# Graph attention and feed-forward, second aggregation: one fp32 product or three products of high and low parts

## The reference

```python
def gat_layer(x, W, att_src, att_dst, bias, src, dst, heads, out_ch, concat):
    h = (x @ W.T).reshape(n, heads, out_ch)
    e = leaky_relu(a_src[src] + a_dst[dst], 0.2)
    ex = jnp.exp(e - segment_max(e, dst)[dst])
    alpha = ex / (segment_sum(ex, dst)[dst] + 1e-16)
    out = segment_sum(alpha[:, :, None] * h[src], dst)
    return out + bias
x = x + gnn(layernorm(x))     # gat 1 (8 x 128), relu, gat 2 (1 x 768)
x = x + ffn(layernorm(x))     # gelu(x @ fc1.T + b) @ fc2.T + b; rows 0 to 5: gated atoms
```

## Time and profile before

| | us |
|---|---|
| median of 3 runs | 778.19 (777.96 to 779.61) |
| profiled execution | 781.36 |
| its span | 779.3 |
| PE busy | 743.4 (95%) |
| DVE busy | 525.1 (67%) |
| ACT busy | 365.4 (47%) |
| POOL busy | 79.1 (10%) |
| granted TensorE clock, mean share of full | 0.989 |

### The profile page before, as it was taken

How to read it: one execution, slowest core, us unless ns; L and a number is a source line. 1 busy time by engine, 2 the same in 40 slices (tenths; PEclk the granted TensorE clock), 3 DMA queues, 4 the chain that set the end, 5 groups by cost and what they waited for, 6 DMA issues and landing times.

```text
span 779.3 us, 12480 instructions
## 1 busy us (share of the span) xinstructions
PE 743.4 (95%) x4367; PEld 629.5 (81%) x4367; DVE 525.1 (67%) x944; ACT 365.4 (47%) x688; POOL 79.1 (10%) x94
## 2 busy tenths in 40 slices
PE   2889999969999999999999899999999999999998
PEld 1769999859899999999999799998567675666755
DVE  6999889498999999999999422253573505813141
ACT  4332434257788888888888811113122222221101
POOL 2011211000000000000000100000322502313010
PEclk9999999998999999999999999999999999999999
DMA  8335656659031112312410130005904038114001
GB/s 295 122 105 150 181 153 196 167 151 339 2 99 34 67 34 66 99 32 67 136 59 0 32 75 1 0 1 165 324 28 142 21 114 281 35 39 163 0 21 60
DMA packets 39770, 78.94 MB, mean 101 GB/s; under 512 B 4057, under 2 KB 25500, under 8 KB 38829
## 3 DMA queue, kind: packets, MB, share of 16 engines
q1 hardware_dynamic: 34057, 60.60, 25.6%
q10 hardware_dynamic: 4484, 13.82, 5.3%
q0 software_dynamic: 1184, 3.92, 2.0%
HBM read 63.04 MB, written 15.29 MB: 101 GB/s over the span
## 4 chain that ended last, share of the span: by engine, by line
PE 92%; DVE 4%; issue 2%; ACT 1%; DVEq 1%; DMA 0%; SPq 0%; ACTq 0%; POOL 0%; POOLq 0%
PE bank L1079 22%; PE bank L1219 17%; PE bank L1060 11%; PE bank L1148 11%; PE bank L992 11%; PE bank L1264 5%; PE bank L1284 4%; PE bank L918 2%; PE bank L1201 1%; PE bank L1095 1%; PE bank L1236 1%; PE bank L1252 1%; PE bank L1299 1%; PE bank L933 1%; PE bank L920 1%
## 5 line engine op out<-in xcount | busy, mean ns | idle before, releaser
L1079 PE MATMUL bank<-PT,h1s 125*128 125x250 f32 x800 | 176.0, 375 | 0.0
L1079 PEld LDWEIGHTS bank<-PT,h1s 125*128 125x128 f32 x800 | 149.0, 190 | 15.6
L1219 PE MATMUL bank<-h,PT 125*125 125x384 f32 x400 | 132.0, 487 | 0.0
L1604 DVE SCALAR_TENSOR_TENSOR L<-asb,nadh 125x1250 f32<-125x1250 f32 x80 | 118.0, 1517 | 7.1 <-PE bank L1060 5.3
L728 ACT COPY PT<-bank 125x500 f32<-125x500 f32 x200 | 100.1, 596 | 40.5 <-PE bank L1060 40.5
L1219 PEld LDWEIGHTS bank<-h,PT 125*125 125x125 f32 x400 | 74.2, 188 | 50.7 <-issue 0.7
L1612 DVE CUSTOM_DVE_ANT_0 L<-L,LC 125x1250 f32<-125x1250 f32 x80 | 113.4, 1456 | 0.0
L715 ACT ACTIVATE L<-L,nm 125x1250 f32<-125x1250 f32 x80 | 107.7, 1370 | 2.1 <-DVE nm L1616 2.1
L1060 PEld LDWEIGHTS bank<-ident,L 125*125 125x125 f32 x800 | 95.4, 192 | 7.5 <-ACT L L715 4.8
L1060 PE MATMUL bank<-ident,L 125*125 125x125 f32 x800 | 96.6, 277 | 4.9 <-ACT L L715 4.6
L1449 DVE TENSOR_TENSOR hotr<-iota,r 125x1500 f16<-125x1500 f16 x50 | 46.7, 935 | 3.1 <-issue 3.1
(11 more groups left out here) (222 smaller groups left out, 1048.1 us busy)
## 6 DMA issues: line engine op xcount, KB each, us to landing
asb<-src_logit_rows SPq DMA_DIRECT2D x7, 1250.0 KB, 6.0
atom_w<-in_atom_inT SPq DMA_DIRECT2D x5, 1152.0 KB, 14.0
atom_w<-in_atom_outT SPq DMA_DIRECT2D x5, 1152.0 KB, 7.5
log_count_scratch<-LCw SPq DMA_DIRECT2D x10, 546.9 KB
LC<-log_count_scratch SPq DMA_DIRECT2D x10, 546.9 KB
LCt<-log_count_scratch SPq DMA_DIRECT2D x10, 546.9 KB
h_scratch<-h1st ACTq DMA_DIRECT2D x10, 448.0 KB
h1s<-h_scratch SPq DMA_DIRECT2D x7, 560.0 KB
```

Of the source, the lines that this page charges most:

```text
L1079: mm = pe.matmul(bank[2 + (k - lag) % 2][:, 0:GW], h1s[q][:, s, :], PT[(k - lag) % 2][:, s, :], start=(s == 0), stop=(s == NT - 1))
L1219: mm = pe.matmul(bank[2 + 2 * j + b][0:NP, 0:HALF], PT5[:, s, j * NP:(j + 1) * NP], h2[:, s, b * HALF:(b + 1) * HALF], start=(s == 0), sto ...
L1604: dve.scalar_tensor_tensor(L[r][:, :], asb[q][0:NP, 1, :], nadh[q][:, t:t + 1], asb[q][0:NP, 0, :], ALU.add, ALU.max).then_inc(stt_done, 1)
```

## The change

The second aggregation is split like the projection. `h2_out` writes `h2_hi` (fp32r, ScalarE, both halves) and `h2_lo` (VectorE, the difference, both halves); `evac_5` writes `PT5_hi`, and VectorE's new `lower_5` writes `PT5_lo` from the same bank. Each (i, j, b) is now ten products high by high, ten high by low, ten low by high (`add_5`, `half_5`); for j = b = 0 they are interleaved with the transposes (`first_half_5`), which use other banks (`T5BANK`). In exchange for the room the low parts take, there is one `LCt` and one `x5` in place of two each, the outputs are summed in place in `x2f` (no `ost`), `tok_y` is gone (gate_logits reads y5), and `gp`, `bo`, `cw` share one place, with pads and other tiles moved. Logits, exponentials, count loads and x5 loads go by tile instead of by group, and stores by tile. `bo` is loaded after five steps of the gate; its bias is added in `gate_weights`, no more in `add_route`. In the diff below, of rewritten functions the new lines stand; the old ones are in the code above.

```diff
-T5BANK = [2, 3, 0, 1, 3]
+T5BANK = [0, 1, 3, 0, 1]
...
-        h2 = sb("h2", [NP, NT, D], F32, two_ctx)
-        PT5 = sb("PT5", [NP, NT, GW], F32, two_ctx)
+        h2_hi = sb("h2_hi", [NP, NT, D], F32R, two_ctx)
+        x5 = sb("x5", [NP, D], F32, two_ctx)
...
-        scr = sb("scr", [NCLS, D], F32, two_ctx)
-        tok_y = sb("tok_y", [NCLS, D], F32, two_ctx)
+        atom_w.append(sb("atom_w2", [128, KD * FH], F32, two_ctx))
+        gT = sb("gT", [128, KF, GW], F32, two_ctx)
...
-        LCt = [sb(f"LCt{j}", [NP, N], F32, p4) for j in range(2)]
+        LCt = sb("LCt", [NP, N], F32, p4)
-        x5 = [sb(f"x5_{j}", [NP, D], F32, p4) for j in range(2)]
+        h2_lo = sb("h2_lo", [NP, NT, D], F32R, p4)
+        PT5_hi = sb("PT5_hi", [NP, NT, GW], F32R, p4)
+        PT5_lo = sb("PT5_lo", [NP, NT, GW], F32R, p4)
-        ost = [sb(f"ost{j}", [NP, D], F32, p4) for j in range(2)]
...
+            def lc_load(n):
+                if n > 0:
+                    sp.wait_ge(max5, n)
+                for a, b in ROWS:
+                    sp.dma_start(LCt[a:b, :], lc_d[n * NP + a:n * NP + b, :]).then_inc(lct_in, 16)
+            def out_store(i, j):
+                first = NCLS if i == j == 0 else 0
+                t = 2 * i + j
+                sp.wait_ge(out_done[j], i + 1)
+                for a, b in ((first, first + CUT), (first + CUT, NP)):
+                    sp.dma_start(out[t * NP + a:t * NP + b, :], x2f[j][a:b, :]).then_inc(out_stored[j], 16)
...
             sp.wait_ge(h2_full, NT)
+            lc_load(2)
             sp.dma_start(b2_sb[:, :], b2.to_broadcast([128, D])).then_inc(bias_in, 16)
             sp.dma_start(fc2b_sb[:, :], fc2b.to_broadcast([128, D])).then_inc(bias_in, 16)
+            sp.dma_start(gp[:, :, :], gate_pair).then_inc(cls_in, 16)
+            sp.dma_start(bal[:, :], balance).then_inc(cls_in, 16)
             sp.dma_start(fc1_sb[:, :, :], fc1T.rearrange("(k p) n -> p k n", p=128)).then_inc(ffn_in, 16)
...
+            lc_load(3)
             for s in range(3):
                 load_atom(s)
...
+            sp.dma_start(fc2_sb[:, :, :], fc2T.rearrange("(k p) n -> p k n", p=128)).then_inc(ffn_in, 16)
+            lc_load(4)
+            sp.wait_ge(gate_step, 5)
             for r, rows in enumerate(([r for _, r in ATOM_SRC], [l for l, _ in ATOM_SRC])):
                 for n in range(0, NCLS):
...
+                    sp.dma_start(bo[n:n + 1, r, :], atom_outb[rows[n]:rows[n] + 1, :]).then_inc(bo_in, 16)
+            lc_load(5)
+            for s in range(3, 5):
                 load_atom(s)
...
+            lc_load(6)
+            out_store(0, 0)
+            out_store(0, 1)
+            lc_load(7)
+            for s in range(5, 8):
                 load_atom(s)
...
+            lc_load(8)
+            out_store(1, 0)
+            out_store(1, 1)
+            lc_load(9)
+            out_store(2, 0)
             for s in range(8, 10):
                 load_atom(s)
...
+            out_store(2, 1)
+            out_store(3, 0)
+            out_store(3, 1)
...
+            def load_x5(n):
                 for a, b in ROWS:
...
+                    pool.dma_start(x5[a:b, :], x[n * NP + a:n * NP + b, :]).then_inc(x5_in, 16)
+            def add_bias(n):
+                pool.wait_ge(x5_in, TWO * (n + 1))
+                pool.tensor_tensor(x5[:, :], x5[:, :], b2_sb[0:NP, :], ALU.add).then_inc(xb_done, 1)
+            def after_x2(n):
+                i, j = n // 2, n % 2
+                pool.wait_ge(x2_done[j], i + 1)
+                if n + 1 < NT:
+                    load_x5(n + 1)
+                pool.wait_ge(ln_step, 3 * n + 3)
+                pool.tensor_tensor(rstd5[j][:, :], var5[j][:, :], powers[:, 0:1], ALU.pow).then_inc(rstd5_ready, 1)
+                if n + 1 < NT:
+                    add_bias(n + 1)
+                if i > 0:
+                    pool.wait_ge(out_stored[j], TWO * i)
+                pool.tensor_tensor(x2f[j][:, :], x2[j][:, :], fc2b_sb[0:NP, :], ALU.add).then_inc(x2f_done[j], 1)
...
-                act.copy(h2[:, ds(2 * i + p, 1), 0:HALF].rearrange("p t n -> p (t n)"),
-                         bank[2 * p][0:NP, 0:HALF]).then_inc(h2a_done, 1)
+                for b in range(2):
+                    c = act.copy(h2_hi[:, ds(2 * i + p, 1), b * HALF:(b + 1) * HALF].rearrange("p t n -> p (t n)"),
+                                 bank[2 * p + b][0:NP, 0:HALF])
+                c.then_inc(h2a_done, 1)
...
+            def exp_5(n):
+                j = n % 2
+                act.wait_ge(nm5_ready, n + 1)
+                act.activation(L5[j][:, :], L5[j][:, :], ACT.Exp, bias=nm5[:, j:j + 1], scale=1.0,
+                               accum_out=den5[:, j:j + 1]).then_inc(exp5, 1)
             def evac_5(i, first=False):
                 for b in range(5):
                     act.wait_ge(t5_full, 5 * i + b + 1)
                     if b == 0 and not first:
                         act.wait_ge(agg5, 2 * i)
...
+                    act.copy(PT5_hi[:, 2 * b:2 * b + 2, :],
+                             bank[T5BANK[b]][0:NP, 0:2 * GW].rearrange("p (s n) -> p s n", s=2)).then_inc(t5_high, 1)
...
+            def turn_5(i, b):
+                if b == 0:
+                    pe.wait_ge(exp5, 2 * i + 2)
+                if b >= 3:
+                    pe.wait_ge(t5_evac, 5 * i + (b - 2))
+                elif i == 0:
+                    pe.wait_ge(h2b_done, NT - 1 if b < 2 else NT)
+                elif b == 2:
+                    pe.wait_ge(x2_done[0], i)
+                elif i > 1:
+                    pe.wait_ge(y_evac, 3 * (i - 1))
+                    pe.wait_ge(hid_done, min(i - 1, 2))
+                    if i == NG - 1 and b == 0:
+                        pe.wait_ge(cand_read, 1)
+                else:
+                    pe.wait_ge(t5_evac, 5 * i)
+                for s in range(2):
+                    for j in range(2):
+                        mm = pe.transpose(bank[T5BANK[b]][0:NP, (2 * s + j) * NP:(2 * s + j + 1) * NP],
+                                          L5[j][:, (2 * b + s) * NP:(2 * b + s + 1) * NP], ident[0:NP, 0:NP])
+                mm.then_inc(t5_full, 1)
...
+            TERMS = {"hh": (PT5_hi, h2_hi), "hl": (PT5_hi, h2_lo), "lh": (PT5_lo, h2_hi)}
+            def add_5(i, j, b, term, sources):
+                rows, features = TERMS[term]
+                for s in sources:
+                    if j == 0 and b == 0 and s % 2 == 0 and term != "hl":
+                        pe.wait_ge(t5_high if term == "hh" else t5_evac, 5 * i + s // 2 + 1)
+                    mm = pe.matmul(bank[2 + 2 * j + b][0:NP, 0:HALF], rows[:, s, j * NP:(j + 1) * NP],
+                                   features[:, s, b * HALF:(b + 1) * HALF], start=(term == "hh" and s == 0),
+                                   stop=(term == "lh" and s == NT - 1))
+                return mm
+            def first_half_5(i):
+                for b in range(3):
+                    turn_5(i, b)
+                if i == 0:
+                    pe.wait_ge(h2a_done, NT)
+                    pe.wait_ge(h2b_done, NT)
+                else:
+                    pe.wait_ge(x2_done[0], i)
+                add_5(i, 0, 0, "hh", range(0, 6))
+                turn_5(i, 3)
+                add_5(i, 0, 0, "hl", range(0, 6))
+                turn_5(i, 4)
+                for term in ("hh", "hl"):
+                    add_5(i, 0, 0, term, range(6, NT))
+                add_5(i, 0, 0, "lh", range(NT))
+            def half_5(i, j, b):
+                if j == 1 and b == 0:
+                    freed(pe, x2_done[1], i)
+                for term in ("hh", "hl", "lh"):
+                    mm = add_5(i, j, b, term, range(NT))
                 if b == 1:
                     mm.then_inc(agg5, 1)
...
+            first_half_5(0)
+            for j, b in ((0, 1), (1, 0), (1, 1)):
+                half_5(0, j, b)
             for i in range(1, NG):
...
+                first_half_5(i)
                 turn_y(i - 1)
...
+                half_5(i, 0, 1)
                 if i == 1:
                     pe.wait_ge(ffn_in, 32)
                 ffn_up(i - 1, part={1: 0, 2: 1}.get(i))
...
+                half_5(i, 1, 0)
                 if i < 3:
                     turn_units(i - 1)
                 ffn_down(i - 1, 0)
                 if i >= 3:
                     candidates(4 - i)
...
+                half_5(i, 1, 1)
                 ffn_down(i - 1, 1)
...
             def h2_out(p, i):
                 t = 2 * i + p
...
+                dve.wait_ge(h2a_done, t + 1)
                 last = bank[2 * p + 1]
                 dve.tensor_copy(as2c[p][:, :], last[0:NP, HALF:HALF + 1])
                 dve.tensor_scalar(nad2[:, ds(t, 1)], last[0:NP, HALF + 1:HALF + 2], SLOPE - 1.0, None, ALU.mult)
...
+                for b in range(2):
+                    c = slice(b * HALF, (b + 1) * HALF)
+                    s = dve.tensor_tensor(h2_lo[:, ds(t, 1), c].rearrange("p t n -> p (t n)"), bank[2 * p + b][0:NP, 0:HALF],
```

(100 more changed lines are left out.)

185 lines of the change are left out of this document (37 added, 148 removed).

## The result

| | before | after |
|---|---|---|
| median, us (9 runs each) | 779.29 | 773.22 |
| lowest to highest | 777.87 to 779.97 | 771.18 to 775.66 |
| profiled execution, its span | 781.36, 779.3 | 772.12, 770.3 |

The ratio is 0.9929, 95% interval 0.9914 to 0.9944: 0.7% faster. The forecast was 872, slower by 94, with 98% on slower. It has the sign wrong.

A forecast was written before the change was run, and what follows sets the result against it. The prediction took TensorE, its matmul side busy 95% of the span, as the bound. Its terms, 82.8 + 2.0 + 3 + 3.3 + 5 = 96 us, were taken as 94: 778.2 + 94 = 872 us, range 860 to 886.

The forecast's parts named there:

- Step 1: Second aggregation's products: 400 fp32 at 0.3225 us (129.0) become 1200 rounded at 0.1765 (211.8), 82.8 us more.
- Rival c: Aggregation products: one fp32 product as dear as four rounded, so three replacing it gain a quarter; 720 us, chance 1%.
- Step 2: Before the stage: h2_out's serial copies and subtractions make TensorE wait about 2.4 and 1.4 us, adding 1.5 and 0.5.
- Step 3: Splitting the transposed rows: subtraction 0.65 to 0.7 us per bank, small copy waits 0.6 per group, 3 us in all.
- Step 4: Group 1, lower_5(1) ahead of norm_5(0, 1) on VectorE: TensorE waits 2 to 3.3 us for y; +3.3 with 0.5 at start.
- Step 5: Groups 2 and 3: GpSimd waits for the output store, delaying VectorE's lower_5 and TensorE, about 2.5 us each, 5 together.
- Step 6: Single LCt and x5, other moved buffers, route biases and the end: no added time, as longer groups cover the loads.

The follow-up runs named there:

- e1: Kernel before with both operands of the second aggregation rounded to fp32r, one product per source tile, low parts left out; 703.09 us, ratio 0.9039.
- e2: Changed kernel with one plain fp32 product of the high parts in place of the three rounded ones, low parts made but unused; 787.40 us, ratio 1.0109.
- e7: Changed kernel with the first layer's aggregation as three rounded 250-column products on the same operands instead of one fp32 product; 768.05 us, ratio 0.9860.
- e5: e3 with the last spread waiting only for the logit column's copy, and the second half's subtraction first, freeing its bank early; 761.34 us, ratio 0.9765.
- e6: e3 with norm_5(0, 1) ahead of lower_5(1) on VectorE in group 1; 766.33 us, ratio 0.9830.
- e3: Changed kernel with out_store(0, 0) and out_store(1, 0) moved ahead of lc_load(6) and lc_load(8) on SP; 762.90 us, ratio 0.9791.
- e4: Changed kernel without the low by high products, low rows still made and waited for; 752.38 us, ratio 0.9661.

## Why the prediction was wrong

**Step 1, the products, failed, and in one factor.** "400 products ... 0.3225 us each" took the number of rows for the number of products. There are 200, of 0.645 us. The old side of the sum, 129.0 us, came out right all the same, as rows times time per row; the new side was then three times 400 instead of three times 200, so 211.8 us stood for 105.4. With 200 the same step gives 105.9 - 129.0 = -23.1. The description of the kernel before had it right, ten fp32 products for each (i, j, b), and two rows already shown had it too: one half in the chain is written x20 where the loop over `NT` makes ten, and the projection's 48 rows per tile are 3 × 8 × 2, one row to a rounded product. e1 and e2 show it from both sides: the type of the operands alone turns 400 rows into 200 and back.

**The rule set aside was right.** The rows show 0.645 us for an fp32 product of 384 columns, 4.03 times 384 columns at 2.4 GHz. The Trainium skill, "FP8 and Floating Point Precision", TensorE Precision Notes, has four passes for true fp32, and by that rule the trace agrees; I had held against it a ratio of 1.83 that was a product against half a product. Rival c, to which I gave 1%, names what happened: its deciding point, put for whole products, is 0.645 / 3 = 0.215 us, and 0.1757 lies under it. Its own price, 70.6 us, was wrong by the same count and by taking a rounded product at a quarter of an fp32 one: it is 3.67 to one.
The columns' cost was right: 0.1757 against 0.1765. The Trainium skill, "TensorE: Matmul & The Clock Gate", Back-to-back issue gap, gave an estimate of 0.1625, by a formula that the section calls the gap of a single matmul and not of a stream with weight loads; the trace is 0.013 above it, and e7 by as much at 250 columns (0.120 for 0.1067).

**Step 2** held: the waits are 2.3 (foreseen 2.4) and 1.3 us (1.4); e5 takes them back in part and gains as much.

**Step 3** held: the subtraction of a bank takes 0.60 to 0.68 us. The small waits for the copy come at two places per group; the weight loads' waits show them in full (TensorE's weight loads from 505 us on), 0.8 per group where 0.6 was foreseen:
```profile
PEld bank L1239 <- ACT PT_hi L837: 4.0, 10, 0.6
```

**Step 4** held in kind and came out smaller: 1.6 us ahead of `turn_y(0)`, foreseen 2 to 3.3. GpSimd's adds did not meet that norm, which took 4.06 us. The 0.5 for group 1's start did not come: its first transposes follow without a wait. e6 shows that the order in the code is the better of the two.

**Step 5** held, link by link, and e3 shows it by taking it away: 5.7 us of waits (3.2 and 2.5, foreseen 5 in all). The store's landing took 4.65 and 4.08 us where about 3 was put. What it left out is the clock: 3.1 us more in slower products behind these waits. I had counted a wait as its length only. The prediction's one example of a longer stall, 4.2 us near the end, was none: the chain of waits goes through VectorE there, but TensorE in order of time has `ffn_down` running beside it and 0.33 us of idle, behind which the clock stays at 1.00. Before, from 745 us on:
```profile
753.91 4.04 PE L1284 MATMUL bank<-fc_sb,gT 128*125 128x384 f32 x12
758.28 1.58 PE L1236 MATMUL bank<-ident,y 125*128 125x125 f32 x12 [0.33 <-DVE y L1762]
```

**Step 6** held as far as the chain shows: no link in it is a load into `LCt` or `x5`. It was not tried with two buffers.

**The sum, redone**, for the two profiled spans. Products -23.6. TensorE's matmul rows wait 10.5 us in the stage (the table above without the spread's 2.3, with 0.7 more for `yT`) where they waited 2.0 before:
```profile
PE bank L1201 <- DVE h L1679: 1.0, 1, 1.0
...
PE bank L1264 <- ACT yT L829: 0.7, 1, 0.7
PE bank L1236 <- DVE y L1762: 0.3, 1, 0.3
```
That is +8.5. Of the waits for the copies the matmul rows show 0.9 and the weight loads 4.0: +3.1. The slower clock: +3.1. Together -8.9. From the last tile's end to the end of the span it was 241.35 us before (779.3 less 537.95) and 232.51 after (770.3 less 537.79): -8.8. Ahead of the stage step 2 adds 1.5 us, and 1.6 us less stand in parts that the change does not touch. Most of that is the clock again. Behind the same wait of 2.47 us, the first 16 products of the second projection took 4.41 us in the profiled execution of before (granted clock 0.58 over the next 3.5 us) and 3.07 in that of the changed kernel (1.00):
```profile
446.29 4.41 PE L1148 MATMUL bank<-w_hi,h1Tt_hi 128*125 128x384 f32 x16 [2.47 <-ACT h1Tt_hi L796]
```
```profile
445.70 3.07 PE L1166 MATMUL bank<-w_hi,h1Tt_hi 128*125 128x384 f32 x16 [2.47 <-ACT h1Tt_hi L809]
```
The span went down by 9.0.

With -23.1 in place of +82.8 and its other terms as they stand, the prediction would have said 766, 7 below the measured 773.2; the slower clock, 3.1 us, is among what it lacked.

## What to carry to other kernels

Before a row count goes into a sum, check it against the loop bounds in the code, once for each type of operand: here an fp32 product is two rows and a rounded one is one. Three fp32r products cost 0.82 of one fp32 product at 384 columns and 0.82 at 250 (0.36 against 0.44 us), provided that somebody has the time to make the low parts and that TensorE is the bound; in e7 70% of such a gain (17.9 of 25.6 us) stayed behind in the layer itself, where VectorE was nearly full. A buffer that is summed in place makes its next writer wait for the store to land: put the store ahead of loads that have time on that queue.

## What the runs showed that was not expected

- A rule and a trace that differ by a factor near two are a reason to recount. Here the factor between the rule's 4 and the 1.83 read was the two rows.
- TensorE's clock after a wait: behind 3.2 us of waiting the granted clock was 0.60 for 3.5 us, so the wait cost about 1.5 us more than its length; behind 2.5 us it was 0.57, with 1.6 us more. It does not follow every such wait. The two rows at 446 us above show both outcomes behind 2.47 us, and behind the same 2.25 us ahead of the last spread the sixteen products of line 1194 took 3.54 us in the changed kernel and 4.99 in e2. Single profiled executions therefore differ by some 1.5 us at one such wait. In e4 and e1, with waits of 5 us, the mean over the span fell to 0.977 and 0.983, where the runs of before on the same chip had 0.991 to 0.996.
- The kernel can be had 2.3% faster than before (e5), of which the change itself is 0.7.
